# A graph layer's tail: one quantising chain over 1536 values per step, and ScalarE's normalising ahead of its copy of q

## The chip, the cores and the metric

The kernel runs on one core of a Trainium2 chip. The metric is the device time of one execution in microseconds (us).

## The reference

`x` has 1250 rows of 1024, with 40000 edges. The layer adds to `x` a graph attention and a linear attention over the normalised rows, and then a feed-forward part whose inputs and weights are rounded to 4-bit values in blocks of 16:

```python
xn = _layernorm(x)
x = x + gnn(xn, edge_index, ...) + mix(xn, ...)
x = x + ffn(_layernorm(x), gate_w, up_w, down_w, s_in, s_in_down)

def fake_quant_nvfp4(x, global_scale):
    xb = x.reshape(sh[:-1] + (sh[-1] // 16, 16))
    amax = jnp.max(jnp.abs(xb), axis=-1, keepdims=True)
    sc8 = jnp.clip(amax / 6.0 * global_scale, 0.0, 448.0).astype(float8_e4m3fn).astype(float32)
    dq = sc8 / global_scale
    a = jnp.clip(jnp.abs(xb) / safe_dq, 0.0, 6.0)
    q = jnp.sign(xb) * _FP4_VALS[jnp.digitize(a, _FP4_MIDS)]
    return (q * dq).reshape(sh)

gate_out, up_out = nvfp4_linear(x, gate_w, s_in), nvfp4_linear(x, up_w, s_in)
hidden = silu(gate_out) * up_out            # 512 wide
return nvfp4_linear(hidden, down_w, s_in_down)
```

So in the feed-forward part 1024 values of each row are quantised before gate and up, and 512 before down.

## The kernel before, in words

The rows are cut into 10 chunks of 128 (C = 10, numbered c = 0 to 9). Up to about 730 us the graph part and the products of the linear attention run; the change does not touch them. The tail, from there to the end, is a software pipeline over steps k = -1 to 12. Each engine has its own loop over k, in an order written out by hand, and the engines meet only in semaphores.

In step k VectorE (DVE) does, in this order:
- the residual additions that `X2_PLAN` puts at (k, 0): L1603, with the bank that PE filled;
- `tail_scales(k)`: the hidden product of chunk k - 1 (L1569: up times silu), its block maximum over 512 values, the block maximum over the 1024 normalised values of chunk k + 1 (both L1258), and the nine small instructions of `scales` (L1223 to L1233) over both parts' blocks at once, 64 + 32 = 96;
- `rows_rounded(k + 1)`: `quantized` over the 1024 values, eight instructions (L1247 to L1255), the last of which writes q of chunk k + 1 and signals `q_done`;
- the additions at (k, 1), then `hidden_rounded(k - 1)`: the same eight instructions over 512 values, which write h of chunk k - 1 and signal `h_done`; then the additions at (k, 2).

Steps -1 and 0 have only the rows, steps 9 and 10 only the hidden part, and steps 1 to 8 both. `finish` (L1608) adds the last chunk's result, which SyncE then stores (L528).

TensorE (PE) in iteration k: `turn_q(k + 1)`, the transposes of q (L927); the up-projection of the attention and, for chunks 7 to 9, the eight products of the base (L905, L908, function `x2`) that are planned at (k, 0); `down(k - 2)`, the transposes of h (L949) and eight matmuls (L960); `gate_up(k + 1)`, sixteen matmuls (L938), which wait for DVE's hidden product of chunk k since it reads the same banks.

ScalarE (ACT) in iteration k: `turn_over(k + 1)`, its copy of the transposed q out of PSUM (L1164); `normalize(k + 2)` (L1023, L1024), which writes the 1024 normalised values for DVE's step k + 1 and needs the root of that chunk's deviation from GpSimd (L714); the copy of h (L1191); `deviation` of chunks that became whole (L1141 to L1146); the silu of chunk k + 1 (L1199) when gate and up are done; `scale_down(k - 2)` (L1156); and deviations of chunks that became whole later in the step.

Normalised rows and silu lie in separate pairs of tiles, and the hidden product in one tile of its own. All of them are parts of `round_mem`, so the profile calls them by that name.

## Time and profile before

| | us |
|---|---|
| median of 3 runs | 914.22 (913.72 to 915.47) |
| the profiled execution, its own time | 911.83 |
| its span | 910.0 |
| PE busy in the span | 857.1 (94%) |
| DVE busy | 818.1 (90%) |
| ACT busy | 550.7 (61%) |
| GpSimd (POOL) busy | 500.0 (55%) |

The span is from the first to the last instruction of one profiled execution; its own time is 1.8 us longer. Busy shares are means over the whole span, and the tail is its last fifth. The timeline views give start and duration of each group of instructions, and in brackets the idle time ahead of it on its engine with what ended it. An instruction's duration reaches a little into the next one's start, so costs are best read from start to start.

### The profile page before, as it was taken

Reading aid. Unit: us, or ns where it says so; the run is one execution under the profiler, and the core shown is the slowest. Engines: PE = TensorE matmul, PEld = TensorE weight load, DVE = VectorE, ACT = ScalarE, POOL = GpSimd, SP = SyncE. Lnnn points to the kernel's source line nnn. Section 1 sums busy time; section 2 is a strip of 40 time slices with the busy share of each in tenths; the row PEclk is TensorE's granted clock in tenths of the full one; section 3 lists DMA queues with packets and bytes.
Section 4 is the critical chain, followed back from the end, with each engine's and each line's share of the span. In section 5 each row is a group of like instructions: output and inputs, shape, how many; then the busy total and the mean of one; then the engine's idle time right before and its main releaser. Section 6 shows DMA issues by size and latency. Waiting matters only on the chain.

```text
span 910.0 us, 9566 instructions
## 1 busy us (share of the span) xinstructions
PE 857.1 (94%) x2744; PEld 419.5 (46%) x2754; DVE 818.1 (90%) x987; ACT 550.7 (61%) x1949; POOL 500.0 (55%) x529
## 2 busy tenths in 40 slices
PE   5999999999999999999999999998999797999755
PEld 5895455644444444444444444443444343444322
DVE  6999996789999999999999999999996069999996
ACT  3313123356677877779898988888998053343342
POOL 3400658577666767877777787877774400010011
PEclk7999999999999999999999999999999899999878
DMA  9322525463655433663336633339939970122224
GB/s 299 109 95 54 173 92 181 142 199 90 81 170 180 103 88 90 193 218 94 101 100 192 193 97 100 101 91 237 356 97 196 191 133 24 63 53 56 39 46 88
DMA packets 73443, 118.37 MB, mean 130 GB/s; under 512 B 29399, under 2 KB 43380, under 8 KB 73370
## 3 DMA queue, kind: packets, MB, share of 16 engines
q0 software_dynamic: 28560, 64.21, 30.5%
q1 hardware_dynamic: 44826, 53.52, 18.3%
q8 instruction: 22, 0.36, 0.2%
q14 instruction: 35, 0.29, 0.1%
HBM read 89.15 MB, written 17.17 MB: 117 GB/s over the span
## 4 chain that ended last, share of the span: by engine, by line
DVE 50%; PE 32%; POOL 7%; issue 6%; DMA 3%; ACT 1%; SPq 0%; ACTq 0%; DVEq 0%; POOLq 0%
PE acc L749 22%; DVE acc_sb L1498 9%; DVE z L1650 9%; DVE turned L1490 8%; DVE turned L1648 8%; POOL round_mem L551 6%; PE turned L905 2%; PE acc L908 1%; DVE round_mem L1258 1%; DVE round_mem L1247 1%; PE acc L938 1%; PE turned L960 1%; DVE big_a L1458 1%; DVE z L1655 1%; DVE round_mem L1248 1%
## 5 line engine op out<-in xcount | busy, mean ns | idle before, releaser
L551 POOL DMA_INDIRECT round_mem<-msg_table,idx x352 | 347.9, 988 | 99.8 <-issue 80.6
L1133 ACT ACTIVATE round_mem<-round_mem,pz 128x65 f32<-128x65 f32 x1408 | 353.9, 398 | 6.4 <-DVE acc_sb L1498 2.5
L749 PE MATMUL acc<-wslot,big_a 128*128 128x512 f32 x512 | 220.3, 592 | 0.0
L749 PEld LDWEIGHTS acc<-wslot,big_a 128*128 128x128 f32 x512 | 97.1, 190 | 121.5 <-issue 121.3
L1498 DVE TENSOR_REDUCE acc_sb<-round_mem 128x260 f32<-128x1820 f32 (+1 forms) x62 | 121.6, 1961 | 7.6 <-ACT round_mem L1133 5.1
L1123 ACT ACTIVATE pz<-z 128x7 f32<-128x7 f32 (+1 forms) x248 | 55.4, 296 | 93.7 <-DVE z L1655 93.4
L749 PE MATMUL acc<-wslot,big_b 128*128 128x512 f32 x256 | 110.0, 592 | 0.0
L749 PE MATMUL acc<-big_b,wslot 128*128 128x512 f32 x256 | 110.0, 592 | 0.0
L1490 DVE TENSOR_TENSOR turned<-round_mem,turned 128x1560 f32<-128x1560 f32 (+1 forms) x62 | 105.4, 1701 | 3.7 <-DMA round_mem<-msg_table,idx 1.6
L1650 DVE TENSOR_REDUCE z<-turned 128x24 f32<-128x1560 f32 (+1 forms) x62 | 105.1, 1695 | 2.1
L1648 DVE SCALAR_TENSOR_TENSOR turned<-turned,att_sb 128x1536 f32<-128x1536 f32 (+1 forms) x62 | 103.5, 1670 | 0.0
L749 PE MATMUL acc<-big_a,xhat_t 128*128 128x512 f32 x224 | 96.6, 593 | 2.7 <-ACT big_a L1070 2.7
L749 PE MATMUL acc<-big_b 128*128 128x512 f32 (+3 forms) x240 | 80.4, 494 | 0.0
L749 PEld LDWEIGHTS acc<-big_b,wslot 128*128 128x128 f32 x256 | 48.6, 190 | 61.2 <-issue 61.0
L749 PEld LDWEIGHTS acc<-wslot,big_b 128*128 128x128 f32 x256 | 48.6, 190 | 61.2 <-issue 61.2
L749 PEld LDWEIGHTS acc<-big_a,xhat_t 128*128 128x128 f32 x224 | 42.4, 190 | 56.9 <-issue 52.4
L714 POOL TENSOR_TENSOR rstd<-small,minus_half 128x1 f32<-128x1 f32 x10 | 6.4, 639 | 98.7 <-ACT small L1146 98.7
L749 PEld LDWEIGHTS acc<-big_b 128*128 128x128 f32 x240 | 42.8, 193 | 35.2 <-issue 29.5
L669 POOL TENSOR_TENSOR round_mem<-acc_sb,pz 128x260 f32<-128x260 f32 x62 | 45.9, 740 | 21.0 <-DVE acc_sb L1498 20.2
L720 POOL DMA_DIRECT2D out_x<-acc_sb x9 | 7.9, 878 | 71.2 <-ACT acc_sb L1156 71.2
L1060 ACT COPY big_a<-acc 128x512 f32<-128x512 f32 x16 | 9.2, 586 | 57.8 <-PE acc L749 42.3
L1199 ACT ACTIVATE round_mem<-acc,cscale 128x512 f32<-128x512 f32 x10 | 6.9, 688 | 59.3 <-PE acc L938 59.3
(233 smaller groups left out, 1031.6 us busy)
## 6 DMA issues: line engine op xcount, KB each, us to landing
round_mem<-msg_table,idx POOLq DMA_INDIRECT x352, 2.8
big_b<-in_x SPq DMA_DIRECT2D x9, 512.0 KB, 8.8
big_b<-big_b SPq DMA_DIRECT2D x9, 512.0 KB, 14.0
big_b<-in_x POOLq DMA_DIRECT2D x9, 512.0 KB, 12.4
out_x<-big_b SPq DMA_DIRECT2D x9, 512.0 KB, 3.6
out_x<-acc_sb POOLq DMA_DIRECT2D x9, 512.0 KB, 5.4
wslot<-in_wv_t SPq DMA_DIRECT2D x2, 2048.0 KB, 10.5
wslot<-in_wk_t SPq DMA_DIRECT2D x2, 2048.0 KB, 9.6
```

Source lines behind the costliest of these rows:

```text
L551: pool.indirect_dma_start(xg[g % 4][:, j, :], None, msg_table, bass.IndirectOffsetOnAxis(idx[:, c, j0 + j:j0 + j + 1], 0)).then_inc(xg_in[ ...
L669: nc.gpsimd.tensor_tensor(halves_of[g % 3][:, :, :, n].rearrange("p i (h d) -> p i h d", d=MR), running[c].rearrange("p (i h d) -> p i h d ...
L749: mm = nc.tensor.matmul(o(acc[:, n % 4, :]), a, b, start=first, stop=last)
L905: nc.tensor.matmul(to, xhat_t[:, k, c * NC:(c + 1) * NC], mat_a[:, k, h * HALF:(h + 1) * HALF], start=(k == 0), stop=False)
L908: mm = nc.tensor.matmul(to, gnn_tr[:, k, c * NC:(c + 1) * NC], wup_sb[:, k, h * HALF:(h + 1) * HALF], start=(c < EARLY and k == 0), stop=( ...
L1060: nc.scalar.copy(mat_a[:, m, h * HALF:(h + 1) * HALF], a).then_inc(t, 1)
L1123: ins = nc.scalar.activation(pz[:, g % 2, 0:slots + 1, h], z[:, g % 3, 0:slots + 1, h], ACT.Exp, scale=-1.0, bias=z[:, (g + 1) % 3, top_sl ...
L1133: ins = nc.scalar.activation(to[:, :, j], xg[g % 4][:, j, h * HR + 1:(h + 1) * HR], ACT.Copy, scale=pz[:, g % 2, j, h:h + 1])
L1490: return nc.vector.tensor_tensor(m4[:, 0:n], xg[g % 4][:, 0:n, :].rearrange("p j (h d) -> p j h d", d=HR)[:, :, :, 0:MR], receiver.unsquee ...
L1498: nc.vector.tensor_reduce(running[c].rearrange("p (i f) -> p i f", i=2), halves_of[g % 3][:, :, :, 0:n + 1], AX.X, ALU.add).then_inc(sum_d ...
L1648: step(nc.vector.scalar_tensor_tensor(m4[:, 0:slots, :, 1:MR], m4[:, 0:slots, :, 1:MR], 0.0, att_sb[0:NC].unsqueeze(1).to_broadcast([NC, s ...
L1650: step(nc.vector.tensor_reduce(zz[:, 0:slots, :], m4[:, 0:slots], AX.X, ALU.add))
```

## The change

Normalised rows and silu of the same step now lie side by side in one slab of 1536 values, two slabs in turn. The hidden product is written in place over the silu. In steps 1 to 8 one block maximum covers all 96 blocks, and `step_rounded(k)` runs the first seven instructions of the chain once over 1536 values. Two multiplications by the scales then write q of chunk k + 1 (1024 wide) and h of chunk k - 1 (512 wide). The waits for PE's transposes of the buffers that are overwritten stand at these two. The residual additions that stood between the two chains follow the whole chain. On ACT `normalize(k + 2)` is called before `turn_over(k + 1)`, and the silu waits for `h_done` in place of `hid_done`. The scratch tiles of the chain are 1536 wide, and some tiles have moved in `round_mem`.

```diff
--- before.py
+++ after.py
@@ -288,20 +288,18 @@
         bias_bc = base[:, C - 1, :]
 
         tail_mem = round_mem
-        silu = [tail_mem[0:NC, i * I:(i + 1) * I] for i in range(2)]
-        ln2 = [tail_mem[0:NC, (1 + i) * D:(2 + i) * D] for i in range(2)]
-        qa = tail_mem[0:NC, 3 * D:4 * D]
-        row_cells, row_steps = (qa[:, i * I:(i + 1) * I].bitcast(BF16) for i in range(2))
-        hidden = tail_mem[0:NC, 4 * D:4 * D + I]
+        NB = (D + I) // QB
+        slab = [tail_mem[0:NC, i * (D + I):(i + 1) * (D + I)] for i in range(2)]
+        ln2, silu = [a[:, 0:D] for a in slab], [a[:, D:D + I] for a in slab]
+        row_cells, row_steps = (tail_mem[0:NC, 6 * I + 768 * i:6 * I + 768 * (i + 1)].bitcast(BF16) for i in range(2))
         q_bf = [tail_mem[0:NC, (9 + i) * I:(10 + i) * I].bitcast(BF16) for i in range(2)]
-        q_t = [tail_mem[:, (11 + i) * I:(12 + i) * I].bitcast(BF16).rearrange("p (k n) -> p k n", k=KB) for i in range(2)]
-        h_bf = [tail_mem[0:NC, 13 * I + i * 256:13 * I + (i + 1) * 256].bitcast(BF16) for i in range(2)]
+        h_bf = [tail_mem[0:NC, 11 * I + i * 256:11 * I + (i + 1) * 256].bitcast(BF16) for i in range(2)]
+        q_t = [tail_mem[:, (12 + i) * I:(13 + i) * I].bitcast(BF16).rearrange("p (k n) -> p k n", k=KB) for i in range(2)]
         h_t = [tail_mem[:, 14 * I + i * 256:14 * I + (i + 1) * 256].bitcast(BF16).rearrange("p (k n) -> p k n", k=4)
                for i in range(2)]
         base_at = [xhat_t[:, :, c * NC:(c + 1) * NC] for c in range(C)]
         gnn_tr = xr_sb[:, :, :].rearrange("p c f -> p (c f)")[:, 0:2 * NP].rearrange("p (k n) -> p k n", k=2)
 
-        NB = (D + I) // QB
         blocks_of = tail_mem[0:NC, 15 * I:15 * I + 8 * NB].rearrange("p (a b) -> p a b", a=8)
         squares = tail_mem[0:NC, 15 * I + 8 * NB:16 * I + 8 * NB].bitcast(BF16)
         tail_max, tail_g = blocks_of[:, 0], blocks_of[:, 1]
@@ -1179,10 +1177,10 @@
             for c in whole[2:]:
                 deviation(c)
             for k in range(-1, C + 2):
+                if 2 <= k + 2 < C:
+                    normalize(k + 2)
                 if 0 <= k + 1 < C:
                     turn_over(k + 1)
-                if 2 <= k + 2 < C:
-                    normalize(k + 2)
                 c = k - 2
                 if 0 <= c < C:
                     act.wait_ge(h_tp, c + 1)
@@ -1195,7 +1193,7 @@
                 if 0 <= c < C:
                     act.wait_ge(gu_full, c + 1)
                     if c >= 2:
-                        act.wait_ge(hid_done, c - 1)
+                        act.wait_ge(h_done, c - 1)
                     nc.scalar.activation(silu[c % 2], acc[0:NC, 2, :], ACT.Silu, scale=cscale[0:NC, 0:1]).then_inc(silu_done, 1)
                 if 0 <= k - 2 < C - 1:
                     scale_down(k - 2)
@@ -1566,30 +1564,42 @@
                 if k - 1 >= 0:
                     c = k - 1
                     dve.wait_ge(silu_done, c + 1)
-                    nc.vector.scalar_tensor_tensor(hidden, acc[0:NC, 3, :], cscale[0:NC, 1:2], silu[c % 2], ALU.mult, ALU.mult).then_inc(hid_done, 1)
+                    nc.vector.scalar_tensor_tensor(silu[c % 2], acc[0:NC, 3, :], cscale[0:NC, 1:2], silu[c % 2], ALU.mult, ALU.mult).then_inc(hid_done, 1)
                     dve.wait_ge(hid_done, c + 1)
-                    ins = block_max(tail_max[:, D // QB:], hidden)
                 if k + 1 < C:
                     dve.wait_ge(ln2_done, k + 2)
-                    ins = block_max(tail_max[:, 0:D // QB], ln2[(k + 1) % 2])
-                step(ins)
+                step(block_max(tail_max[:, lo:hi], slab[(k + 1) % 2][:, lo * QB:hi * QB]))
                 sc8, inv = tail_factors[k % 2]
                 scales(tail_max[:, lo:hi], tail_g[:, lo:hi], (sc8[:, lo:hi], inv[:, lo:hi]),
                        (blocks_of[:, 2, lo:hi], blocks_of[:, 3, lo:hi])).then_inc(tail_scaled, 1)
 
-            def rows_rounded(c):
-                dve.wait_ge(tail_scaled, c + 1)
-                if c >= 2:
-                    dve.wait_ge(q_tp, c - 1)
-                sc8, inv = tail_factors[(c - 1) % 2]
-                quantized(ln2[c % 2], q_bf[c % 2], (sc8[:, 0:D // QB], inv[:, 0:D // QB]), row_cells, row_steps, D).then_inc(q_done, 1)
-
-            def hidden_rounded(c):
-                dve.wait_ge(tail_scaled, c + 3)
-                if c >= 2:
-                    dve.wait_ge(h_tp, c - 1)
-                sc8, inv = tail_factors[(c + 1) % 2]
-                quantized(hidden, h_bf[c % 2], (sc8[:, D // QB:], inv[:, D // QB:]), row_cells[:, 0:I], row_steps[:, 0:I], I).then_inc(h_done, 1)
+            def step_rounded(k):
+
+
+                lo, hi = 0 if k + 1 < C else D // QB, NB if k - 1 >= 0 else D // QB
+                n = hi - lo
+                dve.wait_ge(tail_scaled, k + 2)
+                sc8, inv = (f[:, lo:hi] for f in tail_factors[k % 2])
+                v = slab[(k + 1) % 2][:, lo * QB:hi * QB]
+                by_block = v.rearrange("p (b i) -> p b i", i=QB)
+                high = v.bitcast(U16).rearrange("p (b i t) -> p i b t", i=QB, t=2)[:, :, :, 1]
+                cell, way = row_cells[:, 0:n * QB], row_steps[:, 0:n * QB]
+                step(nc.vector.tensor_tensor(by_block, by_block, inv.unsqueeze(2).to_broadcast([NC, n, QB]), ALU.mult))
+                step(nc.vector.tensor_scalar(cell.bitcast(U16).rearrange("p (i b) -> p i b", i=QB), high, CELL, MIDDLE, ALU.bitwise_and, ALU.bitwise_or))
+                step(nc.vector.tensor_scalar(way.bitcast(U16), cell.bitcast(U16), BINADE, HALF_BIT, ALU.bitwise_and, ALU.bitwise_or))
+                step(nc.vector.tensor_scalar(way, way, 1.5, 64.0, ALU.max, ALU.mult))
+                step(nc.vector.tensor_tensor(cell, cell, way, ALU.add))
+                step(nc.vector.tensor_tensor(way, cell, way, ALU.subtract))
+                step(nc.vector.tensor_scalar(way, way, -FP4_MAX, FP4_MAX, ALU.max, ALU.min))
+                way = way.rearrange("p (i b) -> p i b", i=QB)
+                for there, to, b0, b1, done in ((k + 1 < C, q_bf, 0, D // QB, q_done), (k - 1 >= 0, h_bf, D // QB, NB, h_done)):
+                    if there:
+                        if done is q_done and k >= 1:
+                            dve.wait_ge(q_tp, k)
+                        if done is h_done and k >= 3:
+                            dve.wait_ge(h_tp, k - 2)
+                        nc.vector.tensor_tensor(to[(k + 1) % 2].rearrange("p (i b) -> p i b", i=QB), way[:, :, b0 - lo:b1 - lo],
+                                                sc8[:, b0 - lo:b1 - lo].unsqueeze(1).to_broadcast([NC, QB, b1 - b0]), ALU.mult).then_inc(done, 1)
 
             def residual(c, h):
 
@@ -1673,14 +1683,12 @@
                     residual(*i)
                 if k <= C:
                     tail_scales(k)
-                if 0 <= k + 1 < C:
-                    rows_rounded(k + 1)
+                if k <= C:
+                    step_rounded(k)
                 for i in added_at((k, 1)):
                     residual(*i)
                 if k - 3 == C - 1:
                     finish(k - 3)
-                if 0 <= k - 1 < C:
-                    hidden_rounded(k - 1)
                 for i in added_at((k, 2)):
                     residual(*i)
 
```

In the listings of order the lines of the changed kernel are 2 lower for the same code, up to the new function. DVE, the step that quantises the rows of chunk 6 (k = 5), before: the two maxima, then the chain's first two instructions of each part and its last.

```order
L1258 TENSOR_REDUCE round_mem<-round_mem 128x32 [waits hid_done]
L1258 TENSOR_REDUCE round_mem<-round_mem 128x64 [waits ln2_done]
...
L1233 SCALAR_TENSOR_TENSOR round_mem<-round_mem 128x96 [waits dve_step]
L1247 TENSOR_TENSOR round_mem<-round_mem 128x1024 [waits q_tp,tail_scaled]
L1248 TENSOR_SCALAR round_mem<-round_mem 128x1024 [waits dve_step]
...
L1255 TENSOR_TENSOR round_mem<-round_mem 128x1024 [waits dve_step]
L1603 SCALAR_TENSOR_TENSOR big_b,mean_var<-acc,big_b 128x512 [waits x2_full,x_added9]
L1247 TENSOR_TENSOR round_mem<-round_mem 128x512 [waits h_tp,tail_scaled]
L1248 TENSOR_SCALAR round_mem<-round_mem 128x512 [waits dve_step]
...
L1255 TENSOR_TENSOR round_mem<-round_mem 128x512 [waits dve_step]
```

And in the changed kernel, the same step:

```order
L1256 TENSOR_REDUCE round_mem<-round_mem 128x96 [waits ln2_done,hid_done]
...
L1231 SCALAR_TENSOR_TENSOR round_mem<-round_mem 128x96 [waits dve_step]
L1587 TENSOR_TENSOR round_mem<-round_mem 128x1536 [waits tail_scaled]
L1588 TENSOR_SCALAR round_mem<-round_mem 128x1536 [waits dve_step]
...
L1593 TENSOR_SCALAR round_mem<-round_mem 128x1536 [waits dve_step]
L1601 TENSOR_TENSOR round_mem<-round_mem 128x1024 [waits q_tp,dve_step]
L1601 TENSOR_TENSOR round_mem<-round_mem 128x512 [waits h_tp]
L1613 SCALAR_TENSOR_TENSOR big_b,mean_var<-acc,big_b 128x512 [waits x2_full,x_added9]
```

There is one maximum, which waits for both ln2_done and hid_done, one chain, and the residual addition L1613 stands behind both multiplications L1601.

ACT, from the silu of chunk 3 to the copy of h of chunk 1, before (L1199 silu, L1156 scale_down, L1141 to L1146 deviation, L1164 copy of q, L1023 and L1024 normalising, L1191 copy of h):

```order
L1199 ACTIVATE round_mem<-acc,cscale 128x512 [waits hid_done,gu_full]
L1156 ACTIVATE acc_sb<-turned,cscale 128x1024 [waits gt_tp,down_full]
L1141 ACTIVATE mean_var<-mean_var 128x1 [waits x2_taken]
L1142 ACTIVATE mean_var<-less_mean,mean_var 128x1 [waits act_step]
L1144 ACTIVATE round_mem,mean_var<-big_b,mean_var 128x1024 [waits act_step]
L1146 ACTIVATE small<-mean_var,eps_col 128x1 [waits act_step]
L1164 COPY round_mem<-turned 128x1024 [waits gu_full,q_tp]
L1023 ACTIVATE less_mean<-mean_var,rstd 128x1 [waits q_done,rstd2_done]
L1024 ACTIVATE round_mem<-big_b,less_mean,rstd 128x1024 [waits act_step]
L1191 COPY round_mem<-turned 128x512 [waits h_tp]
```

And in the changed kernel:

```order
L1197 ACTIVATE round_mem<-acc,cscale 128x512 [waits h_done,gu_full]
L1154 ACTIVATE acc_sb<-turned,cscale 128x1024 [waits gt_tp,down_full]
L1139 ACTIVATE mean_var<-mean_var 128x1 [waits x2_taken]
L1140 ACTIVATE mean_var<-less_mean,mean_var 128x1 [waits act_step]
L1142 ACTIVATE round_mem,mean_var<-big_b,mean_var 128x1024 [waits act_step]
L1144 ACTIVATE small<-mean_var,eps_col 128x1 [waits act_step]
L1021 ACTIVATE less_mean<-mean_var,rstd 128x1 [waits q_done,rstd2_done]
L1022 ACTIVATE round_mem<-big_b,less_mean,rstd 128x1024 [waits act_step]
L1162 COPY round_mem<-turned 128x1024 [waits gu_full,q_tp]
L1189 COPY round_mem<-turned 128x512 [waits h_tp]
```

The two normalising instructions (now L1021 and L1022) stand ahead of the copy of q (now L1162), behind the deviation of another chunk.

## Rows read from the trace of the kernel before

**Rows 1.** Busy share in 40 slices of the span, in tenths
```profile
PE   5999999999999999999999999998999797999755
...
DVE  6999996789999999999999999999996069999996
```

**Rows 2.** Windows between L927s: window, length, PE, PEld, DVE, ACT, POOL, PEclk, DMA, GB/s
```profile
772.26:789.28 17.02, 16.97 (x47) 7.85 (x49) 16.16 (x35) 2.45 (x3) 0.00 (x0) 0.83 0.08 32
789.28:805.18 15.90, 14.77 (x56) 6.69 (x56) 15.04 (x33) 7.85 (x16) 1.28 (x2) 1.00 0.25 99
805.18:821.03 15.85, 14.78 (x55) 6.70 (x57) 14.16 (x29) 8.41 (x17) 2.01 (x3) 1.00 0.22 33
821.03:837.19 16.16, 14.98 (x56) 6.75 (x57) 15.30 (x33) 4.72 (x7) 0.89 (x1) 1.00 0.30 66
837.19:852.77 15.58, 14.68 (x56) 6.75 (x57) 14.72 (x31) 6.14 (x11) 1.45 (x2) 1.00 0.23 36
852.77:868.30 15.53, 8.94 (x37) 3.65 (x37) 14.67 (x31) 7.02 (x11) 1.42 (x2) 0.78 0.21 34
868.30:883.21 14.91, 8.41 (x36) 3.49 (x37) 14.05 (x29) 5.61 (x9) 1.91 (x3) 0.77 0.22 35
```

**Rows 3.** Timeline of PE in one iteration; columns: start us, us, engine, line
```profile
801.17 3.62 PE L938 MATMUL acc<-wslot,round_mem 128*128 128x512 bf16 x15
```

**Rows 4.** Timeline of ACT after gate and up
```profile
805.41 1.11 ACT L1156 ACTIVATE acc_sb<-turned,cscale 128x1024 f32<-128x1024 f32 x1
806.40 0.20 ACT L1141 ACTIVATE mean_var<-mean_var 128x1 f32<-128x1 f32 x1
...
808.44 0.99 ACT L1164 COPY round_mem<-turned 128x1024 bf16<-128x1024 bf16 x1
809.33 0.29 ACT L1023 ACTIVATE less_mean<-mean_var,rstd 128x1 f32<-128x1 f32 x1
809.66 1.24 ACT L1024 ACTIVATE round_mem<-big_b,less_mean,rstd 128x1024 f32<-128x1024 f32 x1
```

**Rows 5.** Timeline of DVE, the block maximum over the rows
```profile
810.93 1.22 DVE L1258 TENSOR_REDUCE round_mem<-round_mem 128x64 f32<-128x1024 f32 x1 [0.83 <-ACT round_mem L1024]
```

**Rows 6.** Timeline of DVE, one whole step
```profile
857.61 1.81 DVE L1258 TENSOR_REDUCE round_mem<-round_mem 128x32 f32<-128x512 f32 x2
859.46 0.26 DVE L1223 SCALAR_TENSOR_TENSOR round_mem<-round_mem 128x96 f32<-128x96 f32 x1
...
862.40 1.22 DVE L1247 TENSOR_TENSOR round_mem<-round_mem 128x1024 f32<-128x1024 f32 x1
...
867.55 0.69 DVE L1255 TENSOR_TENSOR round_mem<-round_mem 128x1024 bf16<-128x1024 bf16 x1
868.16 0.68 DVE L1247 TENSOR_TENSOR round_mem<-round_mem 128x512 f32<-128x512 f32 x1
...
871.40 0.43 DVE L1255 TENSOR_TENSOR round_mem<-round_mem 128x512 bf16<-128x512 bf16 x1
```

**Rows 7.** Timeline of POOL in the stretch of rows 4
```profile
808.62 0.56 POOL L714 TENSOR_TENSOR rstd<-small,minus_half 128x1 f32<-128x1 f32 x1 [0.84 <-ACT small L1146]
```

**Rows 8.** Timeline of ACT and of DVE, the last silu and hidden product
```profile
893.32 0.69 ACT L1199 ACTIVATE round_mem<-acc,cscale 128x512 f32<-128x512 f32 x1 [7.95 <-PE acc L938]
...
894.04 0.75 DVE L1569 SCALAR_TENSOR_TENSOR round_mem<-acc,cscale,round_mem 128x512 f32<-128x512 f32 x1
```

**Rows 9.** Timeline of PE, two sets of sixteen L905
```profile
772.26 1.04 PE L927 MATMUL turned<-identb,round_mem 128*128 128x128 bf16 x8 [5.24 <-DVE round_mem L1255]
773.08 9.47 PE L905 MATMUL turned<-big_a,xhat_t 128*128 128x512 f32 x16
...
789.73 7.08 PE L905 MATMUL acc<-big_a,xhat_t 128*128 128x512 f32 x16
```

**Rows 10.** Timeline of PE from 857 us
```profile
857.53 3.59 PE L960 MATMUL turned<-wslot,round_mem 128*128 128x512 bf16 x8 [3.91 <-ACT round_mem L1191]
860.91 4.76 PE L938 MATMUL acc<-wslot,round_mem 128*128 128x512 bf16 x15
```

## The prediction

> **What bounds the kernel now.** I read the busy slices first. VectorE (DVE) stands at 9 in nearly every slice of the last quarter, but TensorE (PE) does too until about 850 us [rows 1]. So the share of busy time does not say which of the two sets the pace there, and the chain of waits alternates between them. I then cut the tail at the starts of PE's transposes of q (L927), one iteration of PE's loop to a window [rows 2]. Four windows, from 789.28 to 852.77, last 15.6 to 16.2 us each. DVE is busy for 14.2 to 15.3 of that and PE for 14.7 to 15.0, and part of PE's missing time is a round trip to ScalarE (ACT) for the copy of h, which recurs in each. From 852.77 on PE has only 8.4 to 8.9 us of work in a window and DVE 14.1 to 14.7: there DVE alone is the bound. One iteration gives its undisturbed length: transposes at 789.28 [rows 2], gate and up from 801.17 for 3.62 [rows 3], so 804.79 - 789.28 = 15.5 us. The next transposes begin only 0.4 us later, at 805.18. **PE has 0.4 us of slack per step there, DVE none to give that PE could use.**
>
> The third view is the path between the two engines. The rows that DVE quantises come from ACT's normalising (L1023, L1024), which stands on ACT's queue behind the silu (L1199), and that waits for PE's gate and up. After gate and up of a step ended at 804.79, ACT ran silu, L1156, a deviation (L1141 to L1146), the copy of q (L1164) and then the normalising, ending at 810.90 [rows 4]. DVE's block maximum over the rows (L1258) waited 0.83 us for it [rows 5].
>
> **The change part by part.** Call q(c) the quantised rows of chunk c, written by L1255 in 1024-wide form.
>
> *Fewer instructions on DVE.* In a step with both parts, the seven instructions L1247 to L1253 over 1024 and the same seven over 512 become seven over 1536. The 1024-wide seven take 867.55 - 862.40 = 5.15 us and the 512-wide seven 871.40 - 868.16 = 3.24 us [rows 6]. If each goes on in a straight line, 1536 costs what 1024 costs plus the difference of 1024 and 512: 5.15 + 1.91 = 7.06, taken as 7.07 us. Saved: 8.39 - 7.07 = 1.32 us, about 0.19 an instruction. The two multiplications by the scale remain, 0.61 and 0.34. The two block maxima (1.81 together) become one of 96 blocks, which I put at 1.79: the pure reduction was already linear. Eight steps have both parts, so DVE has 8 x 1.34 = 10.7 us less to do. The Trainium skill (VectorE: DVE Perf Modes, the section on the fixed extra latency per instruction) gives 58 cycles at 0.96 GHz as the fixed part in its table, and says beside it that about 150 were measured. By the table the merge would save an estimated 8 x 7 x 0.06 = 3.4 us, by the measured figure 8 x 7 x 0.156 = 8.7; the rows say 0.19, and I go by the rows.
>
> *q comes later.* From the start of the block maximum over the rows to the end of q it was 1.25 for the maximum [rows 5], 2.94 for the scales (859.46 to 862.40), 5.15 for the seven and 0.61 for L1255 (867.55 to 868.16, [rows 6]), in all 9.95 us. Now it is 1.79 + 2.94 + 7.07 + 0.61 = **12.4 us, 2.45 us more**. The 512-wide part is finished sooner after q, but nobody waits for that in the middle: PE takes h a whole step later. The single block maximum also waits for the normalised rows, where before the hidden part's reduction ran ahead of that wait.
>
> *ACT's normalising ahead of its copy of q.* That takes L1164's 0.89 us (808.44 to 809.33) off the path where no deviation stands ahead. Where one does, the normalising needs GpSimd's root of that deviation, which ended at 809.18 and had been hidden under L1164 [rows 4, 7]; nothing is won there. So from the end of gate and up to the end of normalising it is 6.1 us with L1156 and a deviation, as measured (5.1 in the one step without L1156), and without deviation 0.62 to the end of the silu, 0.99 for L1156 (805.41 to 806.40) and 1.57 for the normalising (809.33 to 810.90), 3.2 us. The copy of q needs q, which comes later anyway, so its wait behind the normalising costs nothing.
>
> *Waits moved.* The wait for the transposes goes from the head of the chain to its last instructions, and the silu waits for h_done in place of hid_done, one step back. Both were long satisfied: PE's transposes of the buffer in question began a whole step ahead [rows 2], and the h in question ends a step before the silu. Cost 0. No DMA changes.
>
> **The sum.** T(c) is the start of PE's transposes of q(c). It is the later of two: PE's own queue, T(c-1) + 15.5 while the up-projections last; and the path, end of gate and up two chunks back + normalising + 12.4 + 0.1 to PE. The times before are the window edges of [rows 2]:
> T(2): in step 1 of DVE, whose normalised rows are early, 0.02 goes and 1.92 comes ahead of q, so 772.26 + 1.9 = 774.1. The granted clock averaged 0.83 in that window, a mix of 1.2 and 2.4 GHz, and I keep the iteration at its measured 17.0: T(3) = 791.2.
> T(4): path 791.3 + 5.1 + 12.5 = 808.9 against a queue of 806.7. Before: 805.18, so +3.7.
> T(5): path 806.7 + 6.1 + 12.5 = 825.3, queue 824.4. Before 821.03, +4.3. This iteration waits 0.4 more for a residual.
> T(6): queue 841.2, path 824.4 + 3.2 + 12.5 = 840.1. +4.0.
> T(7): path 841.2 + 3.2 + 12.5 = 856.9, queue 856.7. +4.1.
> T(8): path 856.7 + 15.7 = 872.4; before 868.30. +4.1.
> T(9): after normalising (859.9) ACT copies q and then h, 1.5 us, so PE's L960 starts at 861.4; it was 857.53, and gate and up ended 865.67 [rows 10], 8.15 later. So 869.6 + 6.1 + 12.5 = 888.2; before 883.21. **+5.0.**
> From there the end hangs on q(9): transposes, copies, gate and up, and the last silu, which ended as DVE came to the last hidden product at 894.04 with no idle time before it [rows 8]. The two paths were equally long. The new order takes the 512-wide seven, 3.2 us, out of DVE's and leaves DVE waiting for the silu. So the end stays 910.0 - 883.2 = 26.8 us behind T(9): a span of 915.0.
> That is +5.0 on the profiled execution's 911.83 (span 910.0 and 1.8 around it); the three runs' median is 914.22, 2.4 above it. My forecast is 914.22 + 5.0 = **919.2 us**. The same recurrence with 9.95 and L1164 ahead gives T(5) = 804.8 + 6.1 + 10.0 + 0.1 = 821.0 for the kernel before, where 821.03 was measured. Its own range is 916.5 to 921.5: each of the seven hops carries 0.1 to 0.3 us of reading error, and PE's clock is worth 2 either way.
>
> **The rivals.**
> *DVE is the bound and the rest follows.* This is the reading in which the saving counts: steps 1 to 7 each 1.34 shorter, q(9) 1.9 later within its own step, so 914.22 - 7 x 1.34 + 1.9 = **906.7 us**. For it speaks DVE's 9 in every slice; against it that PE had 0.4 us of slack in four of the steps. It decides if a PE iteration is really no longer than DVE's new step, 14.2 to 15.3 less 1.3. 15%.
> *Only PE's queue counts.* If the deviations' path costs less than I read (the normalising waits not arising at T(4) and T(5)), PE runs 1.9 late but without its 0.4 gaps: T(7) is about 853.5, T(9) about 883.5 to 885, and the end **914.5 to 916**. 12%.
> *A colder TensorE.* PE now waits some 2 us before T(4) and 1 before T(5), where it waited 0.4. After 5.24 us of idling before 772.26, and again after 3.91 before 857.53 [rows 10], the windows' granted clock averaged 0.83 and 0.78 [rows 2], and the sixteen L905 that ran from 773.08 took 9.47 in place of 7.08 [rows 9]. One more such stretch costs 2.4: **921.6**, two 924. The Trainium skill (TensorE: Matmul & The Clock Gate, Part 1) says the clock halves after idling and returns under load; by that rule this change, which lengthens idling, is hurt twice. 9%.
> *The wide instructions do not scale.* The multiplication that writes q now reads rows of 64 out of 96. If it lost its speed over L1247's f32 pace it would take that row's 1.22 us for 0.69, some 0.5 more on each of seven paths: **922.5**. Against it: the innermost rows stay contiguous, as before. 4%.
>
> **How the numbers follow.** My forecast has 60%. A measurement of this kernel can tell about 0.2% (1.8 us) from no change. The first rival is faster; of the second I count 2% as faster and 10% as same; my own case and the last two are slower, 60 + 9 + 4: faster 0.17, same 0.10, slower 0.73. The range 912.0 to 922.5 leaves out the first rival and the coldest cases.
>
> **What would show it.** DVE's seven instructions at 7.1 us from the start of the first to the start of L1601; its busy time in the tail about 10.7 us less, and new idle time of some 4 us before the third block maximum, 3 before the fourth and 1 to 2 before later ones, ended by ACT's L1022; PE's transposes of q at about 774, 791, 809, 825, 841, 857, 872, 888; about 3 us of DVE idle before the last hidden product, ended by the silu. I am wrong if the block maximum waits for nobody and PE's transposes come 14 us apart, or if PE's iteration turns out shorter than 15.5.

## The result and the profile after

The changed kernel takes 916.29 us in the median of 20 runs (914.54 to 921.89), the kernel before 913.2 (909.52 to 915.47). The ratio is 1.0046, with a 95% interval of 1.0034 to 1.0058: **slower, by 4.2 us of 913** (the medians alone are 3.1 apart). The profiled execution took 920.49 us, with a span of 918.6, so it lies 4 us above its kernel's median. It is one of the five longest of the twenty, 918.28 to 921.89, and these five have the lowest granted clocks over the whole span, 0.963 to 0.967, where the others have 0.969 to 0.976. The two profiled executions are 8.6 us of span apart, twice what the ratio says, so about half of that is not the change's.

The span and the busy times of the whole execution (columns: engine, us, share, instructions):

```profile
span 918.6 us, 9504 instructions
...
PE 859.4 (94%) x2744; PEld 420.8 (46%) x2754; DVE 809.1 (88%) x923; ACT 551.0 (60%) x1949; POOL 502.7 (55%) x529
```

DVE is busy for 809.1 us where it was 818.1, with 64 instructions less. That is 9.0 us; read from start to start, with the gaps between chained instructions, the saving is larger, as below. PE does the same work. The slices show where DVE's share fell:

```profile
PE   5999999999999999999999999999999796989755
...
DVE  6999996789999999999999999999994179788884
...
PEclk7999999999999999999999999999999997999877
```

The 9s of DVE from 781 us on [rows 1] have become a 7 and 8s. The windows between PE's transposes of q, the same cut and columns as [rows 2]:

```profile
774.74:791.58 16.84, 16.79 (x48) 7.74 (x49) 16.22 (x31) 1.01 (x1) 0.00 (x0) 0.84 0.09 33
791.58:809.35 17.77, 14.78 (x57) 6.70 (x56) 12.70 (x20) 9.73 (x20) 2.37 (x3) 1.00 0.22 89
809.35:826.39 17.04, 16.31 (x55) 7.38 (x57) 13.56 (x22) 6.40 (x12) 1.83 (x3) 0.90 0.21 32
826.39:842.38 15.99, 14.78 (x57) 6.70 (x56) 13.51 (x24) 5.04 (x7) 0.89 (x1) 1.00 0.29 66
842.38:858.26 15.88, 14.66 (x55) 6.84 (x57) 14.04 (x24) 6.08 (x11) 1.50 (x2) 1.00 0.22 34
858.26:874.24 15.98, 8.93 (x37) 3.66 (x36) 13.03 (x22) 7.44 (x11) 1.74 (x2) 0.79 0.22 34
874.24:889.82 15.58, 8.04 (x37) 3.40 (x37) 12.88 (x21) 5.28 (x9) 1.76 (x2) 0.76 0.26 38
```

The first of these starts 2.48 us later than in [rows 2]. Of that, 0.66 us arose before the tail: the first transposes of q, which the change does not touch, began at 749.73, and at 749.07 before. With T(c) for the start of PE's transposes of q(c), as in the prediction, and less those 0.66, T(2) to T(9) were 774.1, 790.9, 808.7, 825.7, 841.7, 857.6, 873.6 and 889.2. Forecast were 774.1, 791.2, 808.9, 825.3, 841.2, 856.9, 872.4 and 888.2.

DVE's instructions that had to wait:

```profile
792.50 0.75 DVE L1567 SCALAR_TENSOR_TENSOR round_mem<-acc,cscale,round_mem 128x512 f32<-128x512 f32 x1 [0.92 <-ACT round_mem L1197]
796.81 1.75 DVE L1256 TENSOR_REDUCE round_mem<-round_mem 128x96 f32<-128x1536 f32 x1 [3.56 <-ACT round_mem L1022]
...
813.17 1.75 DVE L1256 TENSOR_REDUCE round_mem<-round_mem 128x96 f32<-128x1536 f32 x1 [2.89 <-ACT round_mem L1022]
...
829.84 1.75 DVE L1256 TENSOR_REDUCE round_mem<-round_mem 128x96 f32<-128x1536 f32 x1 [1.78 <-ACT round_mem L1022]
...
845.18 1.75 DVE L1256 TENSOR_REDUCE round_mem<-round_mem 128x96 f32<-128x1536 f32 x1 [1.25 <-ACT round_mem L1022]
...
861.71 1.75 DVE L1256 TENSOR_REDUCE round_mem<-round_mem 128x96 f32<-128x1536 f32 x1 [1.78 <-ACT round_mem L1022]
...
877.28 1.75 DVE L1256 TENSOR_REDUCE round_mem<-round_mem 128x96 f32<-128x1536 f32 x1 [2.11 <-ACT round_mem L1022]
...
900.31 0.75 DVE L1567 SCALAR_TENSOR_TENSOR round_mem<-acc,cscale,round_mem 128x512 f32<-128x512 f32 x1 [2.97 <-ACT round_mem L1197]
```

Before, one instruction of these steps waited, 0.83 us [rows 5]. Now six block maxima wait for ACT's normalising, 13.4 us in all, and the last hidden product waits 2.97 us for its silu; two earlier hidden products wait 0.92 (above) and 0.58 us. That is more than the 10.7 us that the merge was to save. The merged chain itself is as short as forecast: from the first of the seven to the multiplications that write q and h it is 773.99 - 766.95 = 7.04 us.

```profile
766.95 1.76 DVE L1587 TENSOR_TENSOR round_mem<-round_mem 128x1536 f32<-128x1536 f32 x1
...
773.99 1.03 DVE L1601 TENSOR_TENSOR round_mem<-round_mem 128x1024 bf16<-128x1024 bf16 x2
```

On ACT the place that answers to [rows 4] shows why moving the normalising forward won nothing behind a deviation:

```profile
807.12 0.69 ACT L1197 ACTIVATE round_mem<-acc,cscale 128x512 f32<-128x512 f32 x1 [3.42 <-PE acc L936]
...
808.70 0.20 ACT L1139 ACTIVATE mean_var<-mean_var 128x1 f32<-128x1 f32 x1
...
811.51 0.29 ACT L1021 ACTIVATE less_mean<-mean_var,rstd 128x1 f32<-128x1 f32 x1 [0.68 <-POOL rstd L712]
811.83 1.24 ACT L1022 ACTIVATE round_mem<-big_b,less_mean,rstd 128x1024 f32<-128x1024 f32 x1
```

From the silu to the end of the normalising it is 811.83 + 1.24 - 807.12 = 5.95 us. Before it was 6.1 from the end of gate and up, with the copy of q in the place where ACT now idles 0.68 us for GpSimd's root.

Four rows of PE show the effect of the granted clock:

```profile
774.74 1.03 PE L925 MATMUL turned<-identb,round_mem 128*128 128x128 bf16 x8 [7.07 <-DVE round_mem L1601]
...
809.80 8.78 PE L903 MATMUL acc<-big_a,xhat_t 128*128 128x512 f32 x16
...
863.05 3.60 PE L958 MATMUL turned<-wslot,round_mem 128*128 128x512 bf16 x8 [3.95 <-ACT round_mem L1189]
...
906.10 3.59 PE L958 MATMUL turned<-wslot,round_mem 128*128 128x512 bf16 x8 [1.25 <-ACT round_mem L1189]
```

After 7.07 us of idling the transposes at 774.74 took 1.03 us, where 0.62 is usual (as at 809.35). The sixteen L903 from 809.80, behind 2.26 us of idling, took 8.78, where 7.08 is the undisturbed value [rows 9], and the granted clock of that window averaged 0.90. The eight L958 at 863.05 were slow before too [rows 10]. Those at 906.10, in the drain of the pipeline (the last steps, in which nothing new enters), took 3.59 as well.

Two of these slow stretches are new against the trace before, and both differ from execution to execution. `merge_not8` below is the changed kernel up to its step 8, and in its profiled execution the sixteen L903 behind the same 2.26 us of idling ran at full length; in those of `merge_only` and `late_q`, behind 2.40 and 2.32 us, they took 8.78 and 8.23, and in no kernel that idles 0.64 us or less there were they slow. So the change makes room for this stretch but does not bring it every time. The one in the drain is not the change's: `act_only` has no merge, and slow matmuls in its drain too:

```profile
809.87 7.08 PE L903 MATMUL acc<-big_a,xhat_t 128*128 128x512 f32 x16
...
898.27 3.59 PE L960 MATMUL turned<-wslot,round_mem 128*128 128x512 bf16 x8 [1.26 <-ACT round_mem L1191]
```

The first of these lines is from `merge_not8`, the second from `act_only`.

### The profile page after: what moved, and what is told of

Same layout as the page of the kernel before. It is cut to its first block, busy times and chain, and to the rows that moved or that the text cites. A ratio compares the mean times of both kernels' runs of the same rounds, so it can differ in the third digit from the quotient of the medians.

```text
span 918.6 us, 9504 instructions
## 1 busy us (share of the span) xinstructions
PE 859.4 (94%) x2744; PEld 420.8 (46%) x2754; DVE 809.1 (88%) x923; ACT 551.0 (60%) x1949; POOL 502.7 (55%) x529
## 4 chain that ended last, share of the span: by engine, by line
DVE 45%; PE 32%; POOL 9%; issue 7%; DMA 4%; ACT 2%; SPq 0%; ACTq 0%; DVEq 0%; POOLq 0%
PE acc L747 21%; DVE acc_sb L1496 8%; DVE z L1660 8%; POOL round_mem L549 8%; DVE turned L1488 8%; DVE turned L1658 7%; PE acc L936 2%; PE turned L958 2%; PE turned L903 2%; PE acc L903 2%; DMA acc_sb<-gnn_dram 2%; PE acc L906 1%; POOL round_mem L667 1%; DVE big_a L1456 1%; DMA big_b<-in_x 1%
```

## The experiments

All ratios are to the kernel before, each timed in five rounds. Where two versions are compared, the difference is that of their ratios, in us of 913, and the figure behind "give or take" follows from the two 95% intervals. Two theories were set against each other. **Path theory:** the loop of gate and up, silu, normalising, DVE's chain up to q and PE's iteration sets the time, and the merge makes it longer. **Work theory:** DVE's busy time sets the pace, and the loss comes from something else, such as the order on ACT or TensorE's clock.

### ACT's order alone (act_only)

```diff
             for k in range(-1, C + 2):
+                if 2 <= k + 2 < C:
+                    normalize(k + 2)
                 if 0 <= k + 1 < C:
                     turn_over(k + 1)
-                if 2 <= k + 2 < C:
-                    normalize(k + 2)
```

> The kernel before with one edit: ACT's normalising ahead of its copy of q. Path theory (the time is set by the loop gate and up, silu, normalising, DVE's chain up to q, PE's iteration): the loop has slack from DVE's own work in the steps without a deviation, so at most 0.5 us faster, ratio 0.9995 to 1.000. Work theory (DVE's busy time sets the pace, and the change was slower for another reason): 0. If this edit were what made the change slower, it would cost 3 to 5 us here (ratio 1.003 to 1.005).

Measured: 912.63 us, ratio 0.999 (0.9975 to 1.0005). It costs nothing and wins nothing that can be told from zero. The loss is in the merge.

### The merge alone (merge_only)

The changed kernel with the diff above undone.

> The changed kernel with ACT's old order (copy of q, then normalising). Path theory: the 2.45 us that q comes later stay, and the steps without a deviation get L1164's 0.89 us of copy back on the path, and more, since the copy waits for the later q: 1 to 3 us slower than the changed kernel, so 5 to 7 us over the kernel before, ratio 1.006 to 1.008. Work theory: as the changed kernel or faster, 1.004 or less.

Measured: 920.83 us, ratio 1.0083 (1.0062 to 1.0103), 3.4 us worse than the change with both edits, give or take 2.2. So the order on ACT is worth something only once q comes late. In the steps without a deviation the maxima wait longer than in the changed kernel:

```profile
830.66 1.75 DVE L1256 TENSOR_REDUCE round_mem<-round_mem 128x96 f32<-128x1536 f32 x1 [2.69 <-ACT round_mem L1022]
...
846.42 1.75 DVE L1256 TENSOR_REDUCE round_mem<-round_mem 128x96 f32<-128x1536 f32 x1 [1.69 <-ACT round_mem L1022]
...
865.13 1.75 DVE L1256 TENSOR_REDUCE round_mem<-round_mem 128x96 f32<-128x1536 f32 x1 [2.69 <-ACT round_mem L1022]
```

These are 2.69, 1.69 and 2.69 us, where the changed kernel's were 1.78, 1.25 and 1.78.

### The same work, q later (late_q)

```diff
-                if 0 <= k + 1 < C:
-                    rows_rounded(k + 1)
+                rows = rows_rounded(k + 1) if 0 <= k + 1 < C else None
+                hid = hidden_rounded(k - 1) if 0 <= k - 1 < C else None
+                if rows:
+                    rows().then_inc(q_done, 1)
...
-                if 0 <= k - 1 < C:
-                    hidden_rounded(k - 1)
+                if hid:
+                    hid().then_inc(h_done, 1)
```

Here `quantized` hands back its last multiplication to be issued later, and the hidden part has scratch tiles of its own.

> The kernel before with the same instructions at the same widths, but in each step with both parts the hidden part's first seven instructions ahead of the multiplication that writes q, which so comes 3.24 us later; DVE does no less and no more work. Path theory: slower, 5 to 11 us (ratio 1.006 to 1.012), more than the changed kernel, since q comes 0.8 us later still and nothing is saved. Work theory: no change, within 1 us.

Measured: 923.0 us, ratio 1.0112 (1.0082 to 1.0142), some 10 us slower. Not an instruction was added and none became longer, so the work theory has no place for it. The residual additions that stood between the two chains come later here too, as in the changed kernel, and no run separates that from the later q; but in this run's trace each of PE's waits for DVE from T(2) to T(9) is ended by q (L1256), and in that of the changed kernel all but one of 0.32 us. DVE waits 1.58 us where it had not, and 2.17 where it had waited 0.83:

```profile
799.28 1.22 DVE L1260 TENSOR_REDUCE round_mem<-round_mem 128x64 f32<-128x1024 f32 x1 [1.58 <-ACT round_mem L1025]
...
816.48 1.22 DVE L1260 TENSOR_REDUCE round_mem<-round_mem 128x64 f32<-128x1024 f32 x1 [2.17 <-ACT round_mem L1025]
```

### Less work, q on time (short_hidden)

```diff
-                step(nc.vector.tensor_scalar(way, way, 1.5, 64.0, ALU.max, ALU.mult))
-                step(nc.vector.tensor_tensor(cell, cell, way, ALU.add))
-                step(nc.vector.tensor_tensor(way, cell, way, ALU.subtract))
+                if not short:
+                    step(nc.vector.tensor_scalar(way, way, 1.5, 64.0, ALU.max, ALU.mult))
+                    step(nc.vector.tensor_tensor(cell, cell, way, ALU.add))
+                    step(nc.vector.tensor_tensor(way, cell, way, ALU.subtract))
```

> The kernel before without three of the hidden part's instructions (L1250, L1251, L1252 at 512 wide) in the eight steps with both parts: the rounding of h is left out there. DVE does 1.25 us less per step, about what the merge saves, and q comes no later within a step. Path theory: 2 to 5 us faster (ratio 0.995 to 0.998), since PE's queue of 15.5 us per iteration takes over in the steps with up-projections and the last gate and up after q(9) keeps its length. Work theory: 8 x 1.25 = 10 us faster, 0.989.

Measured: 909.8 us, ratio 0.9959 (0.9945 to 0.9974), 3.7 us faster of the 10 us that DVE no longer works. The version leaves out three of the instructions that round h, for chunks 0 to 7, so it does not compute the layer; it is here for its time. Most of the relief turns into waits, 6.4 us in all up to the last hidden product, of which the two longest are:

```profile
793.45 1.22 DVE L1259 TENSOR_REDUCE round_mem<-round_mem 128x64 f32<-128x1024 f32 x1 [1.06 <-ACT round_mem L1024]
...
809.80 1.22 DVE L1259 TENSOR_REDUCE round_mem<-round_mem 128x64 f32<-128x1024 f32 x1 [2.56 <-ACT round_mem L1024]
```

So this is what the merge's saving is worth in the kernel before, if it came free: under 4 us.

### The last step's chains apart (merge_not8)

```diff
+            MERGED = (1, 2, 3, 4, 5, 6, 7)
+            def parts(k):
+                lo, hi = 0 if k + 1 < C else D // QB, NB if k - 1 >= 0 else D // QB
+                return [(lo, hi)] if k in MERGED or hi - lo < NB else [(0, D // QB), (D // QB, NB)]
```

`tail_scales` takes the block maxima of each part apart, the hidden one ahead of its wait for the rows, and the loop calls `step_rounded` once per part, with the residual additions of (k, 1) in between.

> The changed kernel with the two chains of step 8 apart, so that the last q comes 2.45 us sooner after the normalised rows; all else as changed. Path theory: T(9) and with it the end 2.4 us earlier than in the changed kernel, though DVE does 1.34 us more: ratio to before 1.001 to 1.003. Work theory: 1.34 us slower than the changed kernel, 1.006.

Measured: 914.68 us, ratio 1.0016 (1.0001 to 1.0031). DVE does more than in the changed kernel, and the time falls by 2.7 us, give or take 1.8: as much as the 2.45 us of q's lateness, in one step. In the two profiled executions T(9) follows T(8) by 12.1 us here and by 15.6 in the changed kernel.

### Deviations ahead of the silu (after_dev, before_dev)

```diff
+                for c in [*whole_at((k, 1)), *whole_at((k, 2))] if k >= 0 else []:
+                    deviation(c)
                 c = k + 1
                 if 0 <= c < C:
                     act.wait_ge(gu_full, c + 1)
...
                 if 0 <= k - 2 < C - 1:
                     scale_down(k - 2)
-                for c in [*whole_at((k, 1)), *whole_at((k, 2))] if k >= 0 else []:
-                    deviation(c)
```

GpSimd's roots move ahead of its `add_to_stored` in the same way. `before_dev` is the kernel before with this and the edit of `act_only`.

> The changed kernel with the deviations of a step's last additions ahead of ACT's silu (and their roots ahead of the store on GpSimd's queue). Their inputs are there long before the silu, so the normalising of chunks 4, 5 and 9 loses 2.9 us of path. Path theory: T(4) 806.7, T(5) 822.4, T(7) 854.0, T(9) 883.1, all the loss but about 1 us is gone: ratio to the kernel before 1.000 to 1.002, against 1.0046 for the change. Work theory and a theory of a colder TensorE alone: no change from the changed kernel, 1.004 to 1.005.

> The kernel before with ACT's normalising ahead of its copy of q and the deviations ahead of the silu, the two edits of ACT alone. In the kernel before DVE's own step (14.2 to 15.3 us) and PE's 15.5 hold the pace and only one wait of 0.8 us came from the normalising, so 0 to 1 us faster: ratio 0.998 to 1.000. If the deviations are worth 5 us in any kernel and not only where q comes late, 0.994.

Measured: `after_dev` 911.15 us, ratio 0.9986 (0.9969 to 1.0004), 5.5 us better than the change, give or take 1.9, and a little better than expected. `before_dev` 911.95 us, ratio 0.9988 (0.997 to 1.0006). The maxima that had waited 3.56 and 2.89 us wait less:

```profile
790.64 1.75 DVE L1256 TENSOR_REDUCE round_mem<-round_mem 128x96 f32<-128x1536 f32 x1 [0.55 <-ACT round_mem L1022]
...
806.99 1.75 DVE L1256 TENSOR_REDUCE round_mem<-round_mem 128x96 f32<-128x1536 f32 x1 [1.78 <-ACT round_mem L1022]
```

The same edit wins 5.5 us where q is late. Where it is not, both edits of ACT together win 1.1 us, and against `act_only` (0.999) the deviations win 0.2; neither can be told from zero. With the deviations off the path the merged and the unmerged kernel take the same time within the 2.3 us that the intervals allow: eight merges, some 10.7 us less work on DVE, and nothing gained or lost that these runs can tell.

### Filling TensorE's idle time (after_warm, before_warm, after_dev_warm)

```diff
+            def keep_busy(n):
+                for _ in range(n):
+                    nc.tensor.matmul(acc[:, 1, :], wgu_sb[:, 0, 0:P], wgu_sb[:, 1, 0:HALF], start=True, stop=True)
...
                 mm.then_inc(h_tp, 1)
+                keep_busy({4: 14, 5: 12, 6: 5, 7: 5, 8: 4, 9: 3}.get(c, 0))
...
                 mm.then_inc(gu_full, 1)
+                keep_busy({7: 9, 8: 9}.get(c, 0))
```

> The changed kernel with idle-filling matmuls on TensorE (bf16, 128x512, into a free bank) after the transposes of h of chunks 4 to 9 and after gate and up of chunks 7 and 8. If a lower granted clock from 857 us on costs the change its time, the L958 that took 3.6 us and the L936 that took 3.7 to 4.8 go back to 1.9 and 3.6, and the end after q(9) shortens by 2 to 5 us: ratio to before 0.999 to 1.003. If the clock is only a side effect, the ratio stays at 1.004 to 1.006.

> The same idle-filling matmuls in the kernel before. There the path from q(9) to the last hidden product and DVE's own work are equally long, so a faster gate and up wins nothing up to 894 us and 0 to 2 us after it: ratio 0.997 to 1.000. If it wins as much as in the changed kernel, the clock's cost is common to both and no part of the difference.

> The changed kernel with both recoveries: deviations ahead of the silu and the idle-filling matmuls. The two took 5.5 and 5.0 us off apart. If they are separate terms (waits from T(4) on, and the clock from 857 us on) they add: ratio to before 0.993 to 0.995. If each only removes the same cold stretches, they do not: 0.998.

Measured: `after_warm` 911.71 us, ratio 0.9991 (0.9976 to 1.0005), 5.0 us better than the change. `before_warm` 910.92 us, ratio 0.9981 (0.9965 to 0.9996), 1.7 us better than the kernel before. So the fillers, 61 matmuls by the code, are worth 3.3 us more in the changed kernel, give or take 2.2. `after_dev_warm` 908.48 us, ratio 0.9954 (0.9937 to 0.9971), 8.4 us better than the change, where 5.5 + 5.0 = 10.5 would be the sum of the two. The 2.1 us between them lie within the 2.8 that the four intervals allow, and the 0.998 that was expected if the two removed the same loss lies outside the interval. The last stretch of the changed kernel (window, length, then the columns of [rows 2]):

```profile
855.00:918.60 63.60, 37.20 (x157) 16.26 (x158) 43.99 (x86) 19.61 (x29) 6.75 (x8) 0.77 0.34 56
```

and with the idle time filled:

```profile
855.00:909.90 54.90, 41.11 (x212) 18.60 (x210) 43.24 (x85) 19.68 (x28) 6.49 (x7) 0.97 0.39 65
```

The granted clock rises from 0.77 to 0.97, and the matmuls that had been slow there are at their undisturbed lengths (1.90 and 3.62, where the kernel before had 3.59 and 4.76 [rows 10]):

```profile
861.13 1.90 PE L964 MATMUL turned<-wslot,round_mem 128*128 128x512 bf16 x8 [0.27 <-ACT round_mem L1195]
862.87 3.62 PE L940 MATMUL acc<-wslot,round_mem 128*128 128x512 bf16 x16
...
889.79 3.62 PE L940 MATMUL acc<-wslot,round_mem 128*128 128x512 bf16 x16
```

The Trainium skill (TensorE: Matmul & The Clock Gate, Part 1) says that the clock halves after idling and returns under load; the trace agrees, with 0.77 against 0.97. The changed kernel is hardly colder than the kernel before, whose last stretch (855 to 910) had 0.79, and `act_only`'s (855 to 911) had 0.74. But more hangs on the clock: after q(9) DVE has 3.2 us less to do, and the gate and up is what the last hidden product waits for (2.97 us above), so each slow matmul there counts, where before it ran beside DVE's own chain.

Where each remedy acts is read from the profiled executions, counted from the transposes of q(0), T(0):

| | T(0) to T(9) | T(9) to the end |
|---|---|---|
| kernel before | 134.14 | 26.79 |
| `act_only` | 134.18 | 29.03 |
| `before_dev` | 133.32 | 27.29 |
| `before_warm` | 134.32 | 25.77 |
| changed kernel | 140.09 | 28.78 |
| `merge_not8` | 135.71 | 27.22 |
| `after_dev` | 132.68 | 29.75 |
| `after_warm` | 137.18 | 24.06 |
| `after_dev_warm` | 134.15 | 23.96 |

Each row is one execution, and the three unmerged rows without fillers differ by 2.2 us behind T(9), so only the large steps count. Moving the deviations takes its 7.4 us ahead of T(9); 1.2 of them are chance, at T(3), where sixteen L903 ahead of the moved work took 8.05 us in place of 9.29. Filling the idle time takes 2.9 us there, 0.8 of which arose before the first filler, and 4.7 behind it. With both remedies both parts are short. And with the idle time filled one sees what the merge does in either part: q(9) comes 2.9 us later than in `before_warm`, and the stretch behind it is 1.7 us shorter, the latter within such scatter.

### Merging where DVE is the bound (merge67_dev, merge67_dev_warm)

`MERGED = (6, 7)`, with both edits of ACT.

> The changed kernel with the merged chain in steps 6 and 7 only, where PE has 8.9 us of work in 15.5 and DVE was the bound, the two chains apart in the other steps, and the deviations ahead of the silu. Path theory: T(2) to T(7) as in the kernel before or up to 1 us earlier, 1.3 to 2.7 us won at T(9): ratio to before 0.996 to 0.999. Work theory: two merges of eight, a quarter of the change's effect, 1.001, if the change's loss comes with the merge.

> Merged chain in steps 6 and 7 only, deviations ahead of the silu, and the idle-filling matmuls. merge67_dev alone stood at 0.994. The clock's part in the kernel before was 1.7 us; if it is worth that or more here: ratio 0.989 to 0.993. If PE's clock no longer matters with DVE as the bound: 0.994.

Measured: `merge67_dev` 907.48 us, ratio 0.9942 (0.992 to 0.9964), 5.3 us faster than the kernel before and the fastest version here; it computes the same. That is better than the 0.996 to 0.999 that were expected, though the interval reaches into them. From T(2) to T(9) DVE never waits (window, length, columns as in [rows 2]):

```profile
771.45:878.70 107.25, 91.91 (x345) 41.72 (x345) 101.69 (x199) 40.89 (x68) 9.33 (x12) 0.93 0.22 50
```

Against `before_dev` that is 4.2 us, where the two merges take 2 x 1.34 = 2.7 off DVE. The two intervals together allow some 2.6 either way, so the 1.5 more cannot be told from zero. In the profiled executions T(0) to T(9) is 130.46 here and 133.32 in `before_dev`, 2.9 us less.

Filling the idle time on top gave 908.22 us, 0.9943 (0.9924 to 0.9961): nothing more. The expected 0.989 to 0.993 was a miss. The fillers were cut to the idle times of other kernels. In this run's trace they hold PE up once: its transposes of q(9) begin 1.15 us after DVE's L1614 does, with no idle time before them, and 0.75 after it in `merge67_dev`. That is 0.4 us of the clock's possible gain; what became of the rest was not tried.

## Why the prediction was right, and where it was off

The time was forecast at 919.2 and measured at 916.29. The forecast +5.0 us stands against +4.2 by the ratio (1.0034 to 1.0058, so 3.1 to 5.3), and the start of the sum, the median of three runs at 914.22, was 1.0 above the median of twenty. The way and the mechanism were right. That the size fits to 0.8 us is in part luck: how much matmuls at the lower clock add differs from run to run, and the sum had no term for that.

- *Fewer instructions on DVE*: 7.07 us for the seven, measured 7.04. Right, and with it that each instruction less saved about 0.19 us.
- *q comes later*, by 2.45 us: right in size, and shown as the cause. `merge_not8` takes one such delay away and wins 2.7 us though DVE works more; `late_q` has a delay of 3.24 us without the saving and loses 10 us.
- *ACT's normalising ahead*: nothing won behind a deviation, 0.89 us elsewhere. Right; `merge_only` shows 3.4 us more loss without it, and `act_only` none with it alone.
- *The sum.* T(2) to T(7) came within 0.7 us of the forecast, T(8) and T(9) 1.2 and 1.0 late. T(4), T(8) and T(9) hung on the path, as forecast. T(5) to T(7) did not come for the reason named: the cold stretch of PE (L903, 8.78) made PE's queue decide at T(5), where the path was forecast, and let the gate and up behind it end later, so that the path decided at T(6), where the queue was forecast, and the queue at T(7). In `merge_not8`, which is the same kernel up to there and had no such stretch, the three were decided as forecast, at 825.5, 841.4 and 857.4 against 825.3, 841.2 and 856.9 (0.30 taken off for its own T(0)).
- *The end stays 26.8 us behind T(9)*: this term was mis-sized for the profiled run. It took 918.6 - 889.8 = 28.8. The last hidden product came 0.3 us sooner behind T(9) than before, and then two sets of eight L958 in the drain took 2.60 and 3.59 where 1.90 is the undisturbed length, 0.7 and 1.7 us. The merge is not what made them slow: `act_only`, without it, took 29.03. The 26.8 were the short end of what the unmerged kernels show.
- *A colder TensorE* had been given 9% as a rival, as an addition of 2.4 us per stretch. It was no rival but a part of the case. The changed kernel is not much colder, but each cold matmul costs it more: filling the idle time takes 5.0 us off it and 1.7 off the kernel before. Filled, the two kernels are 0.9 us apart (ratios 0.9991 and 0.9981), and with the deviations ahead 0.2 (0.9986 and 0.9988), both within the intervals. So either remedy alone takes nearly all of the 4.2 us away, and yet they are in the main two things and not one: together they win 8.4 us, and in the traces one acts ahead of T(9) and the other mostly behind it. How the 4.2 us divide between the waits and the clock stays open, since the kernel before was not run with both remedies. My sum carried the clock only as the measured lengths of the kernel before.
- *DVE is the bound* fell: in `short_hidden` 10 us less work gave 3.7.

## What to carry to other kernels

When two engines hand work to each other around a loop, cost a merge by when its first consumer gets its data, not by the busy time that it saves. Merge a chain where the engine that runs it never waits, so that what is saved in one step counts in the next, here 6 and 7 of eight, and keep the halves apart where the other engine is full or the pipeline drains. Look for work on the path whose inputs are ready long before, like the deviations behind the silu: moving it was worth nothing that could be measured while there was slack, and 5 us when there was none. And before a profiled execution is explained, see where it lies among the runs: here it was one of the five longest of twenty, and a slow stretch in its drain was not the change's doing.

## What the runs showed of the hardware

- A granted clock of 0.77 in the last 64 us of the changed kernel, and of 0.97 in the last 55 with 61 more matmuls in the program, which did no useful work and made it 5 us shorter. In the kernel before the same fillers brought 0.91 from 0.79, and 1.7 us.
- The same sixteen matmuls behind about 7.1 us of idling took 9.29 us in the profiled run of the changed kernel, and 9.47 behind 5.24 us in the kernel before [rows 9]: the longer idling did not make them slower. And behind 2.26 us of idling the same sixteen L903 took 8.78 us in the profiled run of the changed kernel and 7.08 in that of `merge_not8`: the same idling gave a cold stretch in one execution and none in the other.
- A block maximum over 1536 values took 1.75 us, a multiplication over rows of 64 out of 96 (bf16) no more than over whole rows: 0.94 us from start to start for both L1601 together, against 0.61 + 0.34 before.
